# Graph attention edges on one core: the correction two steps earlier, and one wait of ScalarE in place of four

## The chip, the core and the metric

The kernel runs on one core of a Trainium2 chip. It is one program of four graph layers. The metric is the device time of one execution in microseconds; before the change it is 7833.27 us, the median of three runs (7832.72 to 7838.83).

## The reference

A graph has 6250 nodes with 256 features each and 106,250 edges, sorted by destination. Four layers follow one another, each added to its input and normalized: a mean aggregation, a gated recurrent update, a relational layer and an attention layer. The change is in the last, and there in its part over edges. After `qkv = x @ W_qkv`, with 8 heads of 32 features, it computes

```
scores = einsum("phi,phi->ph", q[src], k[dst]) / sqrt(32)
m      = segment_max(scores, src)
e      = exp(scores - m[src])
denom  = segment_sum(e, src)
w      = e / denom[src]
att    = segment_sum(w[:, :, None] * v[dst], src)
```

All data are float32. The division by `denom` comes after the sum: the kernel sums `e * v` and, in a 33rd column of each head, `e`.

## The kernel before

The edges, sorted by their node on the query side, are cut into chunks of 128, and the nodes into windows of 128. A table of 896 entries says for each entry which chunk and which window it joins; below, "chunk c" is entry c. The attention stage works through the chunks, written out without a loop (`walk(..., flat=True)`): each engine has a function `step(c, j, i)`, which is called for every c, with j = c % 32, and does its work at even c for two chunks at once. Each piece of work has a lag: it handles chunk c - lag in step c. The engines run freely and meet by semaphores, so an engine may be some steps ahead of another.

What each engine does in step c:

- ScalarE (`l3_edges_act`): copies the transposed one-hots of c - 4 out of PSUM (L1464), makes the one-hots of c - 2 out of distances (L1470); every fourth chunk copies four index columns for the gathers (L1480) and makes four key columns (L1483); makes the distances of c (L1489).
- GpSimd (`att_gather_pool`): for every chunk one indirect DMA that gathers 128 rows of keys and values, 520 numbers each (L1446). It takes the four index columns as a group. The rows have 32 slots, so chunk c takes the slot of chunk c - 32.
- TensorE (`l3_edges_pe`): transposes the one-hots of c (L1515), multiplies those of c - 2 with the query window, which gives each edge its query (L1524), and sums the weighted values of c - 26 by node with the one-hot (L1550, here called PV).
- VectorE (`l3_edges_dve`): multiplies query and key of c (L1655) and reduces by head (L1680), multiplies values with the weights for c - 22 (L1671), and adds the PV of c - 24 to the running sum of its node window (L1643), once for each of the two chunks (the row named `add`).

The maximum over the edges of a node goes across chunks, so every 16 chunks there is a batch of work on 128 x 128 scores: 16 chunks by 8 heads, transposed (L1542, L1543). VectorE scans them forward and backward (L1581, L1582) in step 0 of a batch, joins the batches by a chain of small operations on one partition in step 2 (L1596 to L1614), scans again with what was carried in and forms the difference `diff` to the maximum in step 4 (L1618 to L1621). ScalarE takes the exponential (L1496) and that of one row which corrects the sum before (L1498). TensorE transposes the exponentials into the weights (L1533) and spreads the row over the partitions by three small matmuls (L1535 to L1537). VectorE reads the weights from its step 6 on (L1671) and the row in step 8 (L1627).

The order on each engine is the order in which the steps are written. A step's waits: GpSimd's gathers of group c wait until the indices are there (`got_idx`) and until VectorE has multiplied the values of the chunks c - 32 to c - 29 (`l3["u"]`), which frees their slots. ScalarE's copy of indices waits for the gathers of the group that used the same index columns (`got3`) and for `gk`; its one-hots wait for the PV of the chunk that used the same place (`l3["pv"]`). The correction on TensorE waits for the exponentials (`p`, `cr`) and for VectorE's last reading of the previous weights (`l3["u"]`).

In the listings below the semaphores have the names under which they were first made: `n0_o` is `p`, `n0_sq` is `w`, `n0_rn` is `cr`, `n0_ss` is `arg`, `n1_aT` is `m`, `n1_hT` is `gk`, `n1_tr` is `pk`; `got_far3` is one of the `got3`.

Of the kernel before, what the change touches and what calls it, by code (L numbers as in the profile page):

```python
# [15 lines left out]
P = 128  # L16
# [3 lines left out]
NT = -(-N_NODES // P)  # L20
# [12 lines left out]
GRP = 4  # L33
# [6 lines left out]
B3 = 16  # L40
N3 = 896
R3 = 32
# [4 lines left out]
HEADS, HD = 8, 32  # L47
# [64 lines left out]
def past(c, n):  # L112

    return not isinstance(c, int) or c >= n
# [7 lines left out]
def program(nc, A, out):  # L122
    with ExitStack() as ctx:
# [1314 lines left out]
        def att_gather_pool(pool):  # L1438
            def step(c, j, i):
                g = j // GRP  # L1440
                if j % GRP == 0:
                    pool.wait_ge(got_idx, i * NG3 + g + 1)
                    if past(c, R3):
                        pool.wait_ge(l3["u"], (c + GRP - R3) // 2)
                    pool.sem_inc(s_pool, 1)
                nc.gpsimd.indirect_dma_start(  # L1446
                    out=rows3(j, 1).rearrange("p s f -> p (s f)"), out_offset=None, in_=kv_d,
                    in_offset=bass.IndirectOffsetOnAxis(ap=gidx[:, g, j % GRP:j % GRP + 1], axis=0)).then_inc(got3[g][0], 16)
            walk(pool, N3, R3, 0, step, flat=True)

        def l3_edges_act(act):
# [4 lines left out]
            def step(c, j, i):  # L1456
# [8 lines left out]
                if live(c, 2, N3):  # L1465
                    u, t, jj = i * (R3 // 2) + (j - 2) // 2, (j - 2) // 2 % 2, (j - 2) % R3
                    act.wait_ge(b3["far"], u + 1)
                    if past(c - 2, R3):
                        act.wait_ge(l3["pv"], u + 1 - R3 // 2)
                    S.activation(oh3[:, jj:jj + 2, :].rearrange("p s n -> p (s n)"), far[:, t, :], ACT.Relu,  # L1470
                                 bias=ones[:, 0:1], scale=-1.0).then_inc(b3["oh"], 1)
                if j % GRP == 0 and live(c, 0, N3):
                    g = j // GRP
                    if past(c, R3):
                        got, base = got3[g]
                        act.wait_ge(got, base + 64 * i)
                        act.wait_ge(b3["gk"], NT + (c - R3) // B3 + 1)
                    of = load_group(mybir.EngineType.Activation, chunk_i, c, GRP, NCK - 1)
                    for a in range(GRP):
                        last = S.copy(gidx[:, g, a:a + 1], idx[:, bass.ds(of[a], 1)])  # L1480
                    last.then_inc(got_idx, 1)
                    for a in range(GRP):
                        last = S.activation(pk[:, j + a:j + a + 1], keyf[:, bass.ds(of[a], 1)], ACT.Identity,  # L1483
                                            bias=nbase[:, bass.ds(c + a, 1)], scale=1.0)
                    last.then_inc(b3["pk"], 1)
                if live(c, 0, N3):
# [1 line left out]
                    for a in range(2):  # L1488
                        last = S.activation(far[:, j // 2 % 2, a * P:(a + 1) * P], iota[:, :], ACT.Abs, bias=pk[:, j + a:j + a + 1], scale=-1.0)  # L1489
                    last.then_inc(b3["far"], 1)  # L1490
                if j % B3 == 10 and batch_at(c, j, i, 10) is not None:
                    b = batch_at(c, j, i, 10)
                    act.wait_ge(b3["m"], NT + b + 1)
                    if past(b, 1):
                        act.wait_ge(b3["w"], NT + b)
                    S.activation(prob, diff, ACT.Exp, scale=SCALE).then_inc(b3["p"], 1)  # L1496
                    act.wait_ge(b3["arg"], NT + b + 1)
                    S.activation(crow, argrow, ACT.Exp, scale=SCALE).then_inc(b3["cr"], 1)  # L1498
            walk(act, N3, R3, 12, step, flat=True)

        def l3_edges_pe(pe):
            T = nc.tensor
# [3 lines left out]
            def step(c, j, i):  # L1506
# [10 lines left out]
                if live(c, 2, N3):  # L1517
# [6 lines left out]
                        last = T.matmul(ps[t][:, a * D:(a + 1) * D], ohT[:, t, a * P:(a + 1) * P],  # L1524
                                        QN[:, bass.ds(at[a], 1), :].rearrange("p a d -> p (a d)"), start=True, stop=True)
                    last.then_inc(l3["q"], 1)
                if j % B3 == 8 and batch_at(c, j, i, 8) is not None:
                    b = batch_at(c, j, i, 8)
                    hot = oh3[0:1, (j - 8 - B3) % R3, :]
                    pe.wait_ge(b3["p"], NT + b + 1)  # L1530
                    if past(b, 1):
                        pe.wait_ge(l3["u"], 8 * b)
                    T.transpose(ps[7][:, 0:P], prob, ident[:, :]).then_inc(b3["w"], 1)  # L1533
                    pe.wait_ge(b3["cr"], NT + b + 1)
                    T.matmul(ps[6][:, 0:HEADS], ones[0:1, :], ones[0:1, 0:HEADS], start=True, stop=False)  # L1535
                    T.matmul(ps[6][:, 0:HEADS], hot, minus, start=False, stop=False)
                    T.matmul(ps[6][:, 0:HEADS], hot, crow, start=False, stop=True).then_inc(b3["corr"], 1)  # L1537
                if j % B3 == 2 and batch_at(c, j, i, 2) is not None:
                    b = batch_at(c, j, i, 2)
                    pe.wait_ge(l3["s"], 8 * (b + 1))  # L1540
# [16 lines left out]
                if j % B3 == 4 and batch_at(c, j, i, 4) is not None:  # L1557
                    pe.wait_ge(b3["car"], NT + batch_at(c, j, i, 4) + 1)
                    pe.sem_inc(s_fill, 1)
                    for k in range(2):  # L1560
                        last = T.transpose(ps[6][:, k:k + 1], car[:, k, :], ident[0:1, 0:1])
                    last.then_inc(b3["col"], 1)
            walk(pe, N3, R3, LAG_PV, step, flat=True)

        def l3_edges_dve(dve, q):
# [498 lines left out]
```

## Time and profile before

| | |
|---|---|
| median of the runs | 7833.27 us |
| profiled execution | 7833.27 us, span 7831.5 us |
| TensorE, matmuls | 5394.5 us busy (69%) |
| VectorE | 5643.8 us busy (72%) |
| ScalarE | 2536.8 us busy (32%) |
| GpSimd | 3719.4 us busy (47%) |
| gathers of the attention stage | 5585.6 to 7287.6 us |
| mean granted TensorE clock | 0.834 |

The shares of the whole span are means over stages with different limits. The attention stage over edges lies between about 5580 and 7341 us. DVE is VectorE, ACT ScalarE, POOL GpSimd, PE TensorE's matmuls and PEld its weight loads; L1550 is line 1550 of the kernel before. In rows of the timeline "x4" is four instructions merged, and the bracket at the end is idle time before the row and what ended it.

### The profile page before, as it was taken

To read this page: it belongs to the slowest core of one execution; us is meant where nothing else is said; L and a number is where in the kernel's file an instruction comes from. 1 tells how busy PE (TensorE), PEld (TensorE's weight loads), DVE (VectorE), ACT (ScalarE), POOL (GpSimd) and SP (SyncE) were. 2 spreads that over 40 slices of the span, in tenths; PEclk is the share of its full clock that TensorE was granted. 3 is DMA by queue.
4 is the path that set the end of the run, shared out by engine and by line. 5 is a ranking of instruction groups with operands and counts; after the bars stand their busy time and mean duration, and the time that the engine had idled before them with its cause. 6 is when DMAs were issued, how large, how long until landed. Compare 5 with 4: busy or idle time off the path is not lost.

```text
span 7831.5 us, 119677 instructions
## 1 busy us (share of the span) xinstructions
PE 5394.5 (69%) x23535; PEld 3797.1 (48%) x23535; DVE 5643.8 (72%) x13697; ACT 2536.8 (32%) x8931; POOL 3719.4 (47%) x3949
## 2 busy tenths in 40 slices
PE   0147777773677767577747777699777777777798
PEld 0024444442344444233336666588655555555587
DVE  6857777736777777476379998711499999999666
ACT  0013323320222323011126666511355555555111
POOL 0057777711777766133347777500245544454111
PEclk9866667796666667688869999999889999999899
DMA  0023333322333333001145555555555555555211
GB/s 11 15 78 99 95 98 100 94 61 67 107 94 98 97 100 96 35 29 34 48 131 157 158 157 155 149 159 161 149 144 143 147 144 144 144 145 144 71 44 36
DMA packets 419172, 810.11 MB, mean 103 GB/s; under 512 B 74474, under 2 KB 267866, under 8 KB 418012
## 3 DMA queue, kind: packets, MB, share of 16 engines
q0 software_dynamic: 191488, 565.92, 26.3%
q1 hardware_dynamic: 224732, 230.95, 9.3%
q10 hardware_dynamic: 2304, 6.29, 0.3%
q8 instruction: 199, 3.26, 0.2%
q14 instruction: 449, 3.68, 0.2%
HBM read 680.15 MB, written 327.48 MB: 129 GB/s over the span
## 4 chain that ended last, share of the span: by engine, by line
PE 34%; DVE 32%; issue 14%; DVEq 5%; POOL 5%; DMA 4%; ACT 3%; SPq 2%; ACTq 1%; POOLq 0%
PE ps L714 7%; PE ps L1324 4%; POOL big L1210 4%; DVEq L194 4%; DVE big L1259 3%; PE ps L1550 3%; PE ps L1524 3%; DVE wreg L1643 3%; DVE ohb L661 3%; DVE big L671 2%; PE ps L1753 2%; PE ps L1770 2%; DVE big L331 2%; DVE big L332 2%; ACT big L457 2%
## 5 line engine op out<-in xcount | busy, mean ns | idle before, releaser
L714 PE MATMUL ps<-ring 128*128 x3528 | 1621.9, 595 | 872.5 <-DVE ohb L661 352.0
L714 PEld LDWEIGHTS ps<-ring 128*128 128x128 f32 x3528 | 781.5, 274 | 1374.7 <-issue 1356.1
L633 POOL DMA_INDIRECT ring<-in_x_dram,idx x832 | 834.0, 1002 | 714.9 <-DVEq L561 370.9
L695 ACT CAST ring<-ohb 128x128 f32<-128x128 bf16 x1764 | 523.4, 298 | 1864.3 <-DVE ohb L661 1830.3
L1446 POOL DMA_INDIRECT ring<-kv_d,gidx x728 | 688.5, 946 | 648.5 <-ACT gidx L1480 468.6
L633 POOL DMA_INDIRECT ring<-x_d,idx x832 | 829.0, 996 | 321.6 <-issue 229.2
L1210 POOL DMA_INDIRECT big<-x_d,idx x832 | 800.0, 962 | 349.1 <-issue 211.2
L1274 PE MATMUL ps<-big,ring 128*128 128x128 f32 x4928 | 734.9, 294 | 297.9 <-DVE big L1249 157.2
L671 DVE TENSOR_TENSOR big<-big,ps 128x257 f32 (+1 forms) x1764 | 756.7, 429 | 252.0 <-issue 87.2
L1274 PEld LDWEIGHTS ps<-big,ring 128*128 128x128 f32 x4928 | 628.7, 194 | 404.1 <-DVE big L1249 307.7
L661 DVE TENSOR_SCALAR ohb<-iotab,keyf,nbase 128x128 bf16<-128x128 bf16 x1764 | 579.8, 329 | 169.3 <-PE ps L718 80.1
L747 POOL TENSOR_TENSOR lns<-lns,neg_half 128x1 f32<-128x1 f32 x294 | 183.3, 623 | 1042.9 <-DVE lns L742 1042.9
L1550 PE MATMUL ps<-big 128*128 128x264 f32 x1792 | 559.3, 439 | 171.6 <-DVE wreg L1643 167.6
L1259 DVE SCALAR_TENSOR_TENSOR big<-big,ps 128x256 f32<-128x256 f32 x1232 | 590.1, 479 | 32.9
L1524 PE MATMUL ps<-big 128*128 x1792 | 546.8, 433 | 24.4 <-issue 8.9
L1235 ACT COPY ring<-big 128x256 f32 x1232 | 415.5, 400 | 332.7 <-POOLq L1199 191.5
L1550 PEld LDWEIGHTS ps<-big 128*128 128x128 f32 x1792 | 343.4, 209 | 346.2 <-issue 305.1
L1643 DVE SCALAR_TENSOR_TENSOR wreg<-wreg,keep,ps 128x264 f32<-128x264 f32 x840 | 402.5, 479 | 33.2 <-PE ps L1550 15.7
L1249 DVE SCALAR_TENSOR_TENSOR big<-iota,small,ring 128x128 f32<-128x128 f32 x1232 | 352.5, 347 | 76.5 <-issue 35.7
L1524 PEld LDWEIGHTS ps<-big 128*128 128x128 f32 x1792 | 348.4, 216 | 92.4 <-issue 57.3
L1324 PE MATMUL ps<-big 128*128 128x256 f32 x1568 | 358.0, 387 | 16.2 <-DMA ring<-x_d 16.2
L1464 ACT COPY big<-ps 128x256 f32<-128x256 f32 x448 | 165.1, 368 | 613.7 <-PE ps L1515 613.3
(328 smaller groups left out, 9502.1 us busy)
## 6 DMA issues: line engine op xcount, KB each, us to landing
bas_d<-big SPq DMA_DIRECT2D x1232, 128.0 KB
att_d<-wreg SPq DMA_DIRECT2D x896, 132.0 KB
big<-bas_d SPq DMA_DIRECT2D x49, 1024.0 KB, 5.6
x_d<-ring SPq DMA_DIRECT2D x147, 128.0 KB, 1.7
ring<-in_x_dram,idx POOLq DMA_INDIRECT x832
ring<-x_d,idx POOLq DMA_INDIRECT x832
big<-x_d,idx POOLq DMA_INDIRECT x832
kv_d<-ring SPq DMA_DIRECT2D x49, 260.0 KB, 2.2
```

Of the source, the lines that this page charges most:

```text
L633: nc.gpsimd.indirect_dma_start(out=rows[:, j, :], out_offset=None, in_=table, in_offset=bass.IndirectOffsetOnAxis(ap=idx_of(c), axis=0)).t ...
L661: V.tensor_scalar(ohb[:, k, :], iotab[:, :], keyf[:, bass.ds(of[k], 1)], nbase[:, q:q + 1], ALU.subtract, ALU.is_equal).then_inc(e["oh"], 1)
L671: V.tensor_tensor(here, here, ps[k][:, 0:width], ALU.add).then_inc(e["acc"], 1)
L714: T.matmul(ps[k][:, 0:D], ohf[:, k, :], rows[:, slot, :].rearrange("p a d -> p (a d)"), start=True, stop=True)
L1210: nc.gpsimd.indirect_dma_start(out=rows2[:, j, :], out_offset=None, in_=x2_d, in_offset=bass.IndirectOffsetOnAxis(ap=idx_of(c), axis=0)).t ...
L1259: V.scalar_tensor_tensor(out=cur[:, k], in0=cur[:, (k - 1) % 8], scalar=keep2[:, bass.ds(cc, 1)], in1=ps[(j - L2_LAG) % 8][:, 0:FW], op0=A ...
L1274: last = nc.tensor.matmul(ps[j % 8][:, 0:FW].rearrange("p (n h b) -> p n h b", n=NB, h=H)[:, :, h, :], xs[:, j, h * P:(h + 1) * P], wts[:, ...
L1324: last = T.matmul(ps[p][:, 0:D], basS[:, p, :, k % H, k // H], bases[:, k // H, k % H, :], start=(k == 0), stop=(k == BASES * H - 1))
L1446: nc.gpsimd.indirect_dma_start(out=rows3(j, 1).rearrange("p s f -> p (s f)"), out_offset=None, in_=kv_d, in_offset=bass.IndirectOffsetOnAx ...
L1524: last = T.matmul(ps[t][:, a * D:(a + 1) * D], ohT[:, t, a * P:(a + 1) * P], QN[:, bass.ds(at[a], 1), :].rearrange("p a d -> p (a d)"), st ...
L1550: last = T.matmul(ps[3 + a][:, 0:AV], oh3[:, jj + a, :], weighted[:, t, a * AV:(a + 1) * AV], start=True, stop=True)
L1643: V.scalar_tensor_tensor(out=acc[:, k], in0=before, scalar=keep[:, bass.ds(y, 1)], in1=ps[3 + a][:, 0:AV], op0=ALU.mult, op1=ALU.add).then ...
```

## The change

Three edits, all in the attention stage over edges.

1. GpSimd's wait for `l3["u"]` is taken out. ScalarE's waits for `got3` and `gk` at the copy of indices are taken out too, and so is the wait for `l3["pv"]` at the one-hots. In their place ScalarE waits, at the copy of indices for group c, for the PV of the chunks up to c - 29.
2. On ScalarE the exponentials are in step 8 of a batch, not in step 10.
3. On TensorE the correction (weights and row) is at the end of step 6 of a batch, not inside step 8.

```diff
--- before.py
+++ after.py
@@ -1440,8 +1440,6 @@
                 g = j // GRP
                 if j % GRP == 0:
                     pool.wait_ge(got_idx, i * NG3 + g + 1)
-                    if past(c, R3):
-                        pool.wait_ge(l3["u"], (c + GRP - R3) // 2)
                     pool.sem_inc(s_pool, 1)
                 nc.gpsimd.indirect_dma_start(
                     out=rows3(j, 1).rearrange("p s f -> p (s f)"), out_offset=None, in_=kv_d,
@@ -1465,16 +1463,12 @@
                 if live(c, 2, N3):
                     u, t, jj = i * (R3 // 2) + (j - 2) // 2, (j - 2) // 2 % 2, (j - 2) % R3
                     act.wait_ge(b3["far"], u + 1)
-                    if past(c - 2, R3):
-                        act.wait_ge(l3["pv"], u + 1 - R3 // 2)
                     S.activation(oh3[:, jj:jj + 2, :].rearrange("p s n -> p (s n)"), far[:, t, :], ACT.Relu,
                                  bias=ones[:, 0:1], scale=-1.0).then_inc(b3["oh"], 1)
                 if j % GRP == 0 and live(c, 0, N3):
                     g = j // GRP
                     if past(c, R3):
-                        got, base = got3[g]
-                        act.wait_ge(got, base + 64 * i)
-                        act.wait_ge(b3["gk"], NT + (c - R3) // B3 + 1)
+                        act.wait_ge(l3["pv"], i * (R3 // 2) + (j + GRP - R3) // 2)
                     of = load_group(mybir.EngineType.Activation, chunk_i, c, GRP, NCK - 1)
                     for a in range(GRP):
                         last = S.copy(gidx[:, g, a:a + 1], idx[:, bass.ds(of[a], 1)])
@@ -1488,15 +1482,15 @@
                     for a in range(2):
                         last = S.activation(far[:, j // 2 % 2, a * P:(a + 1) * P], iota[:, :], ACT.Abs, bias=pk[:, j + a:j + a + 1], scale=-1.0)
                     last.then_inc(b3["far"], 1)
-                if j % B3 == 10 and batch_at(c, j, i, 10) is not None:
-                    b = batch_at(c, j, i, 10)
+                if j % B3 == 8 and batch_at(c, j, i, 8) is not None:
+                    b = batch_at(c, j, i, 8)
                     act.wait_ge(b3["m"], NT + b + 1)
                     if past(b, 1):
                         act.wait_ge(b3["w"], NT + b)
                     S.activation(prob, diff, ACT.Exp, scale=SCALE).then_inc(b3["p"], 1)
                     act.wait_ge(b3["arg"], NT + b + 1)
                     S.activation(crow, argrow, ACT.Exp, scale=SCALE).then_inc(b3["cr"], 1)
-            walk(act, N3, R3, 12, step, flat=True)
+            walk(act, N3, R3, 10, step, flat=True)
 
         def l3_edges_pe(pe):
             T = nc.tensor
@@ -1524,17 +1518,6 @@
                         last = T.matmul(ps[t][:, a * D:(a + 1) * D], ohT[:, t, a * P:(a + 1) * P],
                                         QN[:, bass.ds(at[a], 1), :].rearrange("p a d -> p (a d)"), start=True, stop=True)
                     last.then_inc(l3["q"], 1)
-                if j % B3 == 8 and batch_at(c, j, i, 8) is not None:
-                    b = batch_at(c, j, i, 8)
-                    hot = oh3[0:1, (j - 8 - B3) % R3, :]
-                    pe.wait_ge(b3["p"], NT + b + 1)
-                    if past(b, 1):
-                        pe.wait_ge(l3["u"], 8 * b)
-                    T.transpose(ps[7][:, 0:P], prob, ident[:, :]).then_inc(b3["w"], 1)
-                    pe.wait_ge(b3["cr"], NT + b + 1)
-                    T.matmul(ps[6][:, 0:HEADS], ones[0:1, :], ones[0:1, 0:HEADS], start=True, stop=False)
-                    T.matmul(ps[6][:, 0:HEADS], hot, minus, start=False, stop=False)
-                    T.matmul(ps[6][:, 0:HEADS], hot, crow, start=False, stop=True).then_inc(b3["corr"], 1)
                 if j % B3 == 2 and batch_at(c, j, i, 2) is not None:
                     b = batch_at(c, j, i, 2)
                     pe.wait_ge(l3["s"], 8 * (b + 1))
@@ -1560,6 +1543,17 @@
                     for k in range(2):
                         last = T.transpose(ps[6][:, k:k + 1], car[:, k, :], ident[0:1, 0:1])
                     last.then_inc(b3["col"], 1)
+                if j % B3 == 6 and batch_at(c, j, i, 6) is not None:
+                    b = batch_at(c, j, i, 6)
+                    hot = oh3[0:1, (j - 6 - B3) % R3, :]
+                    pe.wait_ge(b3["p"], NT + b + 1)
+                    if past(b, 1):
+                        pe.wait_ge(l3["u"], 8 * b)
+                    T.transpose(ps[7][:, 0:P], prob, ident[:, :]).then_inc(b3["w"], 1)
+                    pe.wait_ge(b3["cr"], NT + b + 1)
+                    T.matmul(ps[6][:, 0:HEADS], ones[0:1, :], ones[0:1, 0:HEADS], start=True, stop=False)
+                    T.matmul(ps[6][:, 0:HEADS], hot, minus, start=False, stop=False)
+                    T.matmul(ps[6][:, 0:HEADS], hot, crow, start=False, stop=True).then_inc(b3["corr"], 1)
             walk(pe, N3, R3, LAG_PV, step, flat=True)
 
         def l3_edges_dve(dve, q):
```

TensorE, from the end of step 6 of a batch, the kernel before (L1550 is PV, L1515 the transposes of the one-hots, L1524 the query products, L1533 to L1537 the correction):

```order
L1550 MATMUL ps<-big 128x264
L1515 MATMUL ps<-ident,big 128x128 [waits l3_oht,l3_oh]
L1515 MATMUL ps<-ident,big 128x128
L194 TENSOR_LOAD chunk_tab
L1524 ISA [waits l3_prod,l3_oht]
L1524 MATMUL ps<-big 128x256
L1524 ISA
L1524 MATMUL ps<-big 128x256
L1533 MATMUL ps<-ident,wreg 128x128 [waits l3_u,n0_o]
L1535 MATMUL ps<-ones 128x8 [waits n0_rn]
L1536 MATMUL ps<-oh,big 128x8
L1537 MATMUL ps<-big 128x8
```

and the changed kernel (L1533 is now PV, L1552 to L1556 the correction, L1509 the transposes, L1518 the query products):

```order
L1533 MATMUL ps<-big 128x264
L1552 MATMUL ps<-ident,wreg 128x128 [waits l3_u,n0_o]
L1554 MATMUL ps<-ones 128x8 [waits n0_rn]
L1555 MATMUL ps<-oh,big 128x8
L1556 MATMUL ps<-big 128x8
L1509 MATMUL ps<-ident,big 128x128 [waits l3_oht,l3_oh]
L1509 MATMUL ps<-ident,big 128x128
L194 TENSOR_LOAD chunk_tab
L1518 ISA [waits l3_prod,l3_oht]
L1518 MATMUL ps<-big 128x256
L1518 ISA
L1518 MATMUL ps<-big 128x256
```

The correction stood behind the transposes and query products of step 8 and stands ahead of them now.

ScalarE, from the last distances of step 8 of a batch, the kernel before (L1464 copies the transposed one-hots, L1470 makes one-hots, L1489 distances, L1496 and L1498 are the exponentials):

```order
L1489 ACTIVATE ring<-iota,big 128x128
L1464 COPY big<-ps 128x256 [waits l3_q,l3_otr]
L1470 ACTIVATE big<-ring,ones 128x256 [waits l3_pv,l3_far]
L1489 ACTIVATE ring<-iota,big 128x128 [waits n1_tr]
L1489 ACTIVATE ring<-iota,big 128x128
L1496 ACTIVATE wreg<-wreg 128x128 [waits n0_sq,n1_aT]
L1498 ACTIVATE big<-big 1x8 [waits n0_ss]
L1464 COPY big<-ps 128x256 [waits l3_q,l3_otr]
```

and the changed kernel (L1462 copies, L1466 one-hots, L1483 distances, L1490 and L1492 exponentials):

```order
L1483 ACTIVATE ring<-iota,big 128x128
L1490 ACTIVATE wreg<-wreg 128x128 [waits n0_sq,n1_aT]
L1492 ACTIVATE big<-big 1x8 [waits n0_ss]
L1462 COPY big<-ps 128x256 [waits l3_q,l3_otr]
L1466 ACTIVATE big<-ring,ones 128x256 [waits l3_far]
L1483 ACTIVATE ring<-iota,big 128x128 [waits n1_tr]
L1483 ACTIVATE ring<-iota,big 128x128
L1462 COPY big<-ps 128x256 [waits l3_q,l3_otr]
```

The exponentials have moved ahead of the copy, the one-hots and the distances of step 10.

ScalarE, the next copy of indices in a batch (step 12), the kernel before (L194 loads four table values into registers, L1480 copies the index columns):

```order
L1470 ACTIVATE big<-ring,ones 128x256 [waits l3_pv,l3_far]
L194 TENSOR_LOAD chunk_tab [waits n1_hT,got_far3]
L1480 ISA
L1480 COPY gidx<-idx 128x1
L1480 ISA
```

and the changed kernel (L1474 copies the index columns):

```order
L1466 ACTIVATE big<-ring,ones 128x256 [waits l3_far]
L194 TENSOR_LOAD chunk_tab [waits l3_pv]
L1474 ISA
L1474 COPY gidx<-idx 128x1
L1474 ISA
```

The wait for PV has moved from the one-hots to the register load, and the waits for `gk` and the old gathers are gone.

## Rows read from the trace of the kernel before

**Rows 1.** Windows: stretch, length, busy us (instructions) by engine, granted clock, DMA share, GB/s.

```profile
5700.00:7300.00 1600.00, 1187.58 (x4960) 833.36 (x4958) 1481.51 (x3503) 835.38 (x3422) 785.62 (x831) 0.91 0.53 144
6540.00:6545.00 5.00, 4.08 (x11) 3.05 (x12) 3.98 (x13) 1.36 (x4) 1.75 (x2) 0.57 0.60 163
6551.00:6563.00 12.00, 9.32 (x42) 6.68 (x43) 11.73 (x25) 8.24 (x34) 7.56 (x8) 1.00 0.69 196
```

**Rows 2.** Waits of VectorE, 5700 to 7300 us: us in total, times, longest.

```profile
DVE big L1655 <- PE ps L1524: 48.3, 104, 1.3
DVE big L1655 <- DMA ring<-kv_d,gidx: 5.9, 9, 1.2
```

**Rows 3.** Source line of the exponentials: duration min/median/max, first and last start.

```profile
L1496 ACT ACTIVATE wreg<-wreg x56: 309/309/310, 5628.4 to 7309.0; 128x128 f32<-128x128 f32 x56
```

**Rows 4.** Timeline of VectorE in one batch: start, us, engine, line, operation.

```profile
6532.40 0.68 DVE L1655 TENSOR_TENSOR big<-ps,ring 128x512 f32<-128x512 f32 x1
...
6546.38 0.69 DVE L1671 TENSOR_TENSOR big<-big,ps 128x528 f32<-128x528 f32 x1
...
6548.38 0.68 DVE L1655 TENSOR_TENSOR big<-ps,ring 128x512 f32<-128x512 f32 x1
...
6549.78 0.49 DVE L1643 SCALAR_TENSOR_TENSOR wreg<-wreg,keep,ps 128x264 f32<-128x264 f32 x1
...
6551.18 0.68 DVE L1655 TENSOR_TENSOR big<-ps,ring 128x512 f32<-128x512 f32 x1
...
6554.24 0.68 DVE L1655 TENSOR_TENSOR big<-ps,big 128x512 f32<-128x512 f32 x1
...
6557.04 0.68 DVE L1655 TENSOR_TENSOR big<-ps,big 128x512 f32<-128x512 f32 x1
...
6562.80 0.68 DVE L1655 TENSOR_TENSOR big<-ps,ring 128x512 f32<-128x512 f32 x1
```

**Rows 5.** Timeline of TensorE: the same batch.

```profile
6540.90 0.34 PE L1561 MATMUL ps<-ident,iota_q 1*128 1x1 f32 x2 [3.16 <-DVE iota_q L1610]
...
6543.74 1.97 PE L1550 MATMUL ps<-big 128*128 128x264 f32 x4
6545.50 0.64 PE L1515 MATMUL ps<-ident,big 128*128 128x128 f32 x2
6545.93 1.84 PE L1524 MATMUL ps<-big 128*128 x4
6547.61 0.27 PE L1533 MATMUL ps<-ident,wreg 128*128 128x128 f32 x1
...
6548.61 1.13 PE L1550 MATMUL ps<-big 128*128 128x264 f32 x4
6549.57 0.38 PE L1515 MATMUL ps<-ident,big 128*128 128x128 f32 x2
6549.79 1.03 PE L1524 MATMUL ps<-big 128*128 x4
...
6554.47 1.13 PE L1550 MATMUL ps<-big 128*128 128x264 f32 x4 [0.82 <-DVE wreg L1643]
```

**Rows 6.** Timeline of ScalarE in the same batch.

```profile
6546.50 0.31 ACT L1496 ACTIVATE wreg<-wreg 128x128 f32<-128x128 f32 x1 [3.24 <-DVE wreg L1621]
...
6547.48 0.45 ACT L1480 COPY gidx<-idx 128x1 int32 x4
```

**Rows 7.** Chain that ended last, around one late group of gathers: start, us, what.

```profile
6644.24 0.31 ACTq L194
...
6644.80 0.09 ACT gidx L1480
...
6649.81 4.58 DMA ring<-kv_d,gidx
```

**Rows 8.** Timeline at the start of the stage: a last gather, VectorE's next product.

```profile
5599.40 0.94 POOL L1446 DMA_INDIRECT ring<-kv_d,gidx  x1 [0.30 <-issue]
...
5603.22 0.69 DVE L1655 TENSOR_TENSOR big<-ps,ring 128x512 f32<-128x512 f32 x1 [1.59 <-DMA ring<-kv_d,gidx]
```

## Prediction

> **What bounds the kernel now.** Read the windows of the attention stage first. Between 5700 and 7300 us VectorE is busy for 1481.5 of 1600 us, TensorE for 1187.6, ScalarE for 835.4, GpSimd for 785.6, and the DMA engines for about half of the time [rows 1]. VectorE bounds the stage, by some 93%. The waits say how much a better order could give: in these 1600 us VectorE waited 48.3 us for the query products (L1524) and 5.9 us for gathered rows [rows 2]. Only the stage is touched: its 56 batches start 1680.6 us apart from first to last, 30.6 us each [rows 3]. I work on one batch, from VectorE's product at 6532.40 us to the one at 6562.80 us, 30.40 us, close to that mean [rows 4].
>
> A word on names. "Step c" is what an engine does for loop index c, two chunks at a time, and c is counted from the batch's start (0, 2, ... 14, then 16 = the next 0). VectorE's product of step c needs the query product of c, which TensorE makes in its step c+2. VectorE's first accumulate of step c needs the value product ("PV") of TensorE's step c+2. The "correction" is the transpose of the probabilities and the three small matmuls (L1533 to L1537 of before).
>
> In the batch, step 6 of VectorE starts at 6548.38, its first accumulate at 6549.78, and steps 8, 10, 12 and 16 start at 6551.18, 6554.24, 6557.04 and 6562.80 [rows 4].
>
> **The correction, two steps earlier on TensorE and ScalarE.** First what releases it. ScalarE's exponential starts at 6546.50, after a wait for VectorE's difference, not for its own queue [rows 6]. All 56 of them have to wait for that, and moving the exponential ahead in ScalarE's queue can't start it earlier. The transpose also waits for VectorE to have read the previous batch's weights, the multiply of step 4, which runs from 6546.38 to 6547.07 [rows 4]. So in the new order too the correction can't start before 6547.07.
>
> Today TensorE uses that waiting time: in step 8 it does the one-hot transposes (6545.50) and the query products (6545.93, 1.84 us), then the correction at 6547.61, then PV at 6548.61 [rows 5]. In the new order the correction stands ahead of those two. TensorE ends the PV of step 6 at 6545.71 [rows 5], stands still until 6547.07, and does the correction in 1.0 us (6547.61 to 6548.61 today) until 6548.1. Only then come transposes and query products. They take 1.25 us at the full clock (6549.57 to 6550.82) or 2.27 us at the half clock (6545.50 to 6547.77) [rows 5]. ScalarE's new order doesn't hold them up further: today too the exponentials are followed by a copy and a one-hot, and it is through with those at 6547.48, when the copy of indices starts [rows 6].
>
> So VectorE's product of step 6 starts at 6549.35 or 6550.4 instead of 6548.38. What counts is the first accumulate. At the full clock PV runs from about 6549.2 for 1.13 us, VectorE needs 1.2 us for product and multiply, and the accumulate is at 6550.6, against 6549.78: 0.8 us later. At the half clock the PV takes 2.0 us [rows 5] and ends at 6552.2: 2.4 us later. Which clock? TensorE had stood still for 3.16 us until 6540.90 [rows 5], and the granted clock from 6540 to 6545 was 0.57 of full, that is mostly the 1.2 GHz level; from 6551 to 6563 it was 1.00, that is 2.4 GHz [rows 1]. The new order adds an idle stretch of 1.4 us where the clock is just coming back, so both will be seen. I take the middle, 1.6 us a batch, and keep 0.8 and 2.4 as ends. In 56 batches: 90 us (45 to 134). Nothing behind it absorbs it: the correction feeds the accumulate of step 8, which VectorE reaches later anyway.
>
> **The gather's gate.** GpSimd no longer waits for the multiply that frees a row slot, and ScalarE's index copy for group c (chunks c to c+3) now waits for a PV. Both guard the same chunks, c-32 to c-29. But the multiply of c-30 is VectorE's step c-8, while its PV is TensorE's step c-4. The gate opens some four to six chunks later. Behind the waiting instruction in ScalarE's queue are the keys, the distance and one-hot of the next chunks, behind them in GpSimd's the four gathers.
>
> How long from gate to data? The chain of one group where the data came late: register load at 6644.24, index copy at 6644.80, the last of the four gathers issued at 6649.81, landed 4.58 us later: 10.15 us from load to landing [rows 7]. At the start of the stage a last gather, issued at 5599.40, let VectorE go on at 5603.22, after 3.82 us [rows 8]. With 3.82 it is 9.4 us, with 0.1 us to pass the semaphore 9.5. I take 9.5, and keep 9.1 (a landing 0.4 us quicker than that row) and 10.25 (the slow group).
>
> The Trainium skill, page "DMA: Bandwidth & Descriptors", section "Anatomy of one DMA — SWDGE (gpsimd) path", fits 2.0 us plus the bytes at 436 GB/s for a GpSimd DMA; for the 260 KB of one gather that is an estimate of 2.6 us. The trace disagrees (3.82 and 4.58); by the page each group would be there 1.2 us sooner and the term below would fall to some 60 us. The skill's page "Runtime: NRT & Kernel Launch", section "Instruction fetch mechanics", gives about 200 ns for each register loaded; by it the four registers of a group cost 0.8 us, an estimate, where the trace shows 0.56 us from the load to the copy [rows 7], and the term would grow by some 13 us.
>
> Now against the need, group by group. Group 16: its gate is the PV of step 12, which starts 0.23 us after VectorE's product of step 10 (6554.24 and 6554.47) and takes 1.13 us [rows 4, 5]. Its data are there 1.36 + 9.5 = 10.86 us after that product. VectorE wants them at 6562.80, 8.56 us after it. Missing: 2.3 us. Group 12: its gate is the PV of step 8, whose end is at the first accumulate of step 6 or up to 0.2 us ahead; from there to the product of step 12 are 7.26 us (6549.78 to 6557.04) [rows 4], up to 7.5, against 9.5. Missing: 2.1 us. The two are not added: a stall before step 12 also gives group 16 its time, so both together cost 2.3 us. Groups 4 and 8 have the long chain steps 0 to 6 of VectorE ahead (6532.40 to 6551.18 is 18.8 us for eight chunks) and are in time. With 9.1 us it is 1.9, with 10.25 it is 3.05. The first 32 chunks have no gate, so 54 batches: 124 us (103 to 165). This hides what VectorE waits for gathers today, 5.9 us in the window [rows 2], about 7 in the stage.
>
> **Sum.** 90 + 124 - 7 = 207 us on a span of 7831.5 gives 8038.5. The median of the runs is 7833.27, 1.8 us above the profiled span, so the forecast is 8040 us. The terms do add: the correction delays the PV that opens gate 12, it doesn't overlap with the time behind it. By the ends of both terms: 45 + 103 - 7 = 141 and 134 + 165 - 7 = 292, so 7974 to 8125; a half-speed PV at the gates would add up to 0.9 us in a batch, hence 8150 as the upper end.
>
> **Rivals.**
> 1. Only the correction costs; the gathers are in time after all, because their landing is nearer 2 us where the queue is not full, or because VectorE's own delay gives them room. For it: VectorE waited for gathers only 9 times on ring slots in 1600 us [rows 2]. Against: these waits come with a gate that opens four chunks sooner. 7833 + 90 = 7923 us.
> 2. Only the gate costs; the correction finds idle time, TensorE runs fast, and VectorE's first accumulate, which waits for PV anyway, moves by nothing. For it: it holds if the query product of step 6 were ready before the correction's releaser; against: it stands behind it in the queue. 7833 + 117 = 7950 us.
> 3. No change: both waits were implied by others. For it: PV of the same chunks was already waited for by ScalarE in its next step but one or so (L1470). Against: that wait asks for two chunks fewer and two steps earlier work. 7833 us.
> 4. Faster. The mechanism is in steps 6 to 8: with the correction out of TensorE's step 8 its PV follows the query products at once, and VectorE's waits for L1524 shrink. It decides if the correction's operands are ready before TensorE has ended step 6. The price is bounded by the waits, 48.3 us [rows 2]; if half of them went, and all of the 7 us for gathers with GpSimd's freed wait, that is 31 us: 7802 us. Against it is the difference that releases the exponential, later than the end of step 6 in the row.
>
> **How the numbers follow.** Both costs 0.68; rival 1 0.09; rival 2 0.08; rival 3 0.07; rival 4 0.08. What this kernel's measurement can tell from no change is about 0.2%, 16 us. Slower by over 0.2%: 0.68 + 0.09 + 0.08 = 0.85; within: 0.07; faster: 0.08. The likeliest case's own range is 7970 to 8150. To hold the time 8 times in 10 I extend it down to 7915, which takes in rivals 1 and 2.
>
> **What the changed profile would show.** Right: on TensorE the correction's transpose waits over 1 us for ScalarE or VectorE in most batches, with the one-hot transposes and query products right behind it; VectorE waits for L1518 at step 6; new VectorE waits for gathered rows of about 2 us once in a batch, at chunk 12 (and little at 16); GpSimd waits for the index copy, ScalarE's register load for PV; a batch of 34.3 us. Its busy times stay. Wrong: if VectorE's waits for gathers stay at a few us, the gate's term is gone; if the product of step 6 follows its predecessor without a wait, the correction's term is gone. Wrong in size: a landing time near 2 us, or a TensorE clock that stays at one level in steps 6 to 8.

## The result and the profile after

The changed kernel takes 8121.76 us (8115.53 to 8129.23, 4 runs) against 7836.05 us for the kernel before, measured with it: ratio 1.0361, 95% interval 1.0342 to 1.0379. By the medians that is 286 us slower; 207 us were forecast, and the forecast of 8040 us is 82 us short. The span of the profiled execution is 8115.3 us.

The busy times of the stage have not changed, only its length. Windows of the changed kernel, from 5700 us until nearly all chunks are through (answers to rows 1; columns as there):

```profile
5700.00:7560.00 1860.00, 1331.84 (x4930) 904.48 (x4928) 1482.62 (x3483) 836.87 (x3430) 792.41 (x832) 0.85 0.45 123
```

VectorE's 1482.62 us are the 1481.51 of rows 1, but in 1860 us and not 1600. The exponentials' source line (answers to rows 3):

```profile
L1490 ACT ACTIVATE wreg<-wreg x56: 309/309/310, 5623.6 to 7592.0; 128x128 f32<-128x128 f32 x56
```

(7592.0 - 5623.6) / 55 is 35.8 us a batch, against 30.6: 5.2 us more. The waits of the changed kernel, 5700 to 7570 us (answers to rows 2; total us, times, longest; L1518 makes the query products, L1533 is PV, L1552 the correction's transpose):

```profile
ACT gidx L1474 <- PE ps L1533: 553.2, 209, 4.3
...
DVE big L1649 <- PE ps L1518: 206.7, 217, 2.9
...
PE ps L1552 <- DVE big L1665: 85.9, 52, 2.1
...
DVE big L1649 <- DMA ring<-kv_d,gidx: 65.7, 69, 2.1
...
DVE big L1649 <- DMA big<-kv_d,gidx: 39.3, 26, 2.3
...
PE ps L1509 <- ACT big L1466: 24.7, 73, 0.6
```

VectorE waits 206.7 us for query products (48.3 before) and 105.0 us for gathered rows (6.6 before, both kinds of slots). The correction waits for VectorE, as forecast, and ScalarE waits 553.2 us at its new gate. The last row is new too: TensorE waits for one-hots (L1466) behind that gate, 24.7 us in 73 times, a wait that the kernel before does not have between 5700 and 7300 us. One batch on VectorE, in the timeline of the changed kernel (answers to rows 4; steps 2, 4, 6, the first accumulate of step 6, steps 8, 10, 12, 14 and 16):

```profile
6512.21 0.69 DVE L1649 TENSOR_TENSOR big<-ps,ring 128x512 f32<-128x512 f32 x1 [0.18 <-PE ps L1518]
...
6519.62 0.69 DVE L1649 TENSOR_TENSOR big<-ps,ring 128x512 f32<-128x512 f32 x1 [0.68 <-PE ps L1518]
...
6526.08 0.69 DVE L1649 TENSOR_TENSOR big<-ps,ring 128x512 f32<-128x512 f32 x1 [2.05 <-PE ps L1518]
...
6527.82 0.49 DVE L1637 SCALAR_TENSOR_TENSOR wreg<-wreg,keep,ps 128x264 f32<-128x264 f32 x1 [0.44 <-PE ps L1533]
...
6529.22 0.68 DVE L1649 TENSOR_TENSOR big<-ps,ring 128x512 f32<-128x512 f32 x1
...
6532.85 0.69 DVE L1649 TENSOR_TENSOR big<-ps,ring 128x512 f32<-128x512 f32 x1 [0.49 <-PE ps L1518]
...
6537.02 0.69 DVE L1649 TENSOR_TENSOR big<-ps,ring 128x512 f32<-128x512 f32 x1 [1.48 <-DMA ring<-kv_d,gidx]
...
6539.64 0.68 DVE L1649 TENSOR_TENSOR big<-ps,ring 128x512 f32<-128x512 f32 x1
...
6542.85 0.69 DVE L1649 TENSOR_TENSOR big<-ps,ring 128x512 f32<-128x512 f32 x1 [0.18 <-DMA ring<-kv_d,gidx]
```

Read the brackets: 2.05 us for the product of step 6 and 0.44 us for the PV behind it, then 0.49 us for the product of step 10, and 1.48 and 0.18 us for gathered rows at steps 12 and 16. TensorE in the same batch (answers to rows 5):

```profile
6522.79 0.30 PE L1552 MATMUL ps<-ident,wreg 128*128 128x128 f32 x1 [1.68 <-DVE big L1665]
...
6523.48 0.36 PE L1556 MATMUL ps<-big 1*128 1x8 f32 x2
6523.78 0.44 PE L1509 MATMUL ps<-ident,big 128*128 128x128 f32 x2
6524.07 1.97 PE L1518 MATMUL ps<-big 128*128 x4
6525.83 1.95 PE L1533 MATMUL ps<-big 128*128 128x264 f32 x4
```

The correction starts at 6522.79 and takes 1.0 us, as at the full clock in rows 5. The query product follows it, at 6524.07, in 1.97 us: the half clock. And the gate: ScalarE's copy of indices and GpSimd's first and fourth gather of group 12.

```profile
6528.23 0.47 ACT L1474 COPY gidx<-idx 128x1 int32 x4 [3.20 <-PE ps L1533]
...
6529.51 0.94 POOL L1444 DMA_INDIRECT ring<-kv_d,gidx  x1 [9.50 <-ACT gidx L1474]
...
6533.25 0.95 POOL L1444 DMA_INDIRECT ring<-kv_d,gidx  x1 [0.30 <-issue]
```

PV ended at 6527.78 (6525.83 + 1.95), the rows were there at 6537.02: 9.24 us, where I took 9.5.

### The profile page after: what moved, and what is told of

It reads as the page before. It is cut to its first block, busy times and chain, and to the rows that moved or that the text cites. A ratio compares the mean times of both kernels' runs of the same rounds, so it can differ in the third digit from the quotient of the medians.

```text
span 8115.3 us, 119026 instructions
## 1 busy us (share of the span) xinstructions
PE 5523.2 (68%) x23532; PEld 3865.2 (48%) x23535; DVE 5655.8 (70%) x13697; ACT 2539.4 (31%) x8931; POOL 3722.7 (46%) x3949
## 3 DMA queue, kind: packets, MB, share of 16 engines
q0 software_dynamic: 191488, 565.92, 25.2%
## 4 chain that ended last, share of the span: by engine, by line
PE 33%; DVE 30%; issue 13%; DMA 6%; POOL 5%; DVEq 5%; ACT 4%; SPq 2%; ACTq 1%; POOLq 0%
PE ps L714 6%; PE ps L1324 4%; PE ps L1518 4%; DVE big L1259 4%; DVEq L194 4%; POOL big L1210 3%; DVE ohb L661 3%; DMA ring<-kv_d,gidx 2%; DVE big L671 2%; PE ps L1747 2%; PE ps L1764 2%; PE ps L1533 2%; DVE big L331 2%; POOL ring L1444 2%; DVE big L332 2%
## 5 line engine op out<-in xcount | busy, mean ns | idle before, releaser
L1533 PE MATMUL ps<-big 128*128 128x264 f32 x1792 | 597.9, 465 | 135.3 <-DVE wreg L1637 131.2
L1518 PE MATMUL ps<-big 128*128 x1792 | 605.8, 471 | 61.5 <-issue 37.8
L1533 PEld LDWEIGHTS ps<-big 128*128 128x128 f32 x1792 | 384.8, 229 | 309.4 <-issue 247.3
L1649 DVE TENSOR_TENSOR big<-ps,ring 128x512 f32<-128x512 f32 x364 | 251.2, 690 | 308.1 <-PE ps L1518 213.2
L1518 PEld LDWEIGHTS ps<-big 128*128 128x128 f32 x1792 | 376.3, 233 | 159.7 <-issue 118.0
L1637 DVE SCALAR_TENSOR_TENSOR wreg<-wreg,keep,ps 128x264 f32<-128x264 f32 x840 | 402.7, 479 | 37.4 <-PE ps L1533 35.3
```

Source lines behind the costliest of these rows:

```text
L1533: last = T.matmul(ps[3 + a][:, 0:AV], oh3[:, jj + a, :], weighted[:, t, a * AV:(a + 1) * AV], start=True, stop=True)
```

## The experiments

Theory A is the prediction's: two costs, the order of the correction on TensorE and the late gate, here with the sizes read from the trace after. Differences in us are the change of the ratio times 7834 us, with the 95% interval of the ratio; differences of the medians lie up to 7 us from them (e1 +190, e2 +138). "Us a batch" is read from the first and last start of the exponentials, as in rows 3; it was 30.6 before.

| kernel | against before | ratio | us a batch |
|---|---|---|---|
| changed kernel | +283 | 1.0342 to 1.0379 | 35.8 |
| correction alone (e1) | +197 | 1.0234 to 1.0268 | 33.9 |
| gate alone (e2) | +143 | 1.0166 to 1.0200 | 33.0 |
| gate opened by the multiply (e3) | 0 | 0.9991 to 1.0010 | 30.5 |
| correction on TensorE alone (e4) | +187 | 1.0222 to 1.0257 | 34.0 |
| exponentials on ScalarE alone (e5) | +256 | 1.0309 to 1.0344 | 35.3 |
| GpSimd waits for PV (e6) | +76 | 1.0080 to 1.0113 | 31.9 |
| changed kernel, gaps filled (e7) | +178 | 1.0210 to 1.0244 | 33.7 |
| before, gap filled (e8) | -11 | 0.9976 to 0.9996 | 30.3 |
| e1, gaps filled (e9) | +31 | 1.0025 to 1.0052 | 31.2 |
| carries later (e10) | +5 | 0.9999 to 1.0016 | 30.6 |
| carries and rows later (e11) | +1 | 0.9992 to 1.0009 | 30.7 |
| e10, gaps filled (e12) | -20 | 0.9960 to 0.9987 | (other chip) |

**The correction alone (e1).** Edits 2 and 3 of the change without edit 1.

> The kernel before with the correction moved on TensorE and ScalarE alone; all waits of the gathers as before. Theory A (two costs that add; in the trace of the changed kernel VectorE waits about 2.05 us for the query product of step 6 and 0.44 us for the PV behind it, at the half clock, in every batch): +2.5 us in each of 56 batches, about +140 us, and hardly any wait of VectorE for gathers. Theory B (the gate is the main cost, the correction is slow only because ScalarE and TensorE are already late from the gate): under +60 us.

Measured +197 us: neither theory's number, though the place is A's. VectorE waits 215.0 us for query products over the whole stage (57.7 before) and 31.5 us for gathers (31.1 before). VectorE in one batch of e1 (the multiply of step 4, the product of step 6, its first accumulate, the product of step 8):

```profile
6539.97 0.69 DVE L1671 TENSOR_TENSOR big<-ring,ps 128x528 f32<-128x528 f32 x1
...
6544.99 0.69 DVE L1655 TENSOR_TENSOR big<-ps,ring 128x512 f32<-128x512 f32 x1 [2.94 <-PE ps L1524]
...
6546.75 0.49 DVE L1643 SCALAR_TENSOR_TENSOR wreg<-wreg,keep,ps 128x264 f32<-128x264 f32 x1 [0.46 <-PE ps L1539]
...
6548.47 0.69 DVE L1655 TENSOR_TENSOR big<-ps,ring 128x512 f32<-128x512 f32 x1 [0.23 <-PE ps L1524]
```

and TensorE (L1558 to L1562 are the correction, L1539 PV), with the windows of the stretch from the carries' transposes to the half-speed products (the granted clock is the third number from the end):

```profile
6540.81 0.45 PE L1558 MATMUL ps<-ident,wreg 128*128 128x128 f32 x1 [1.51 <-DVE big L1671]
...
6542.06 0.57 PE L1562 MATMUL ps<-big 1*128 1x8 f32 x2
6542.56 0.69 PE L1515 MATMUL ps<-ident,big 128*128 128x128 f32 x2
6543.04 1.91 PE L1524 MATMUL ps<-big 128*128 x4
6544.75 1.97 PE L1539 MATMUL ps<-big 128*128 128x264 f32 x4
```

```profile
6534.50:6546.90 12.40, 10.88 (x31) 7.99 (x32) 7.99 (x20) 4.24 (x18) 2.29 (x3) 0.50 0.24 71
```

The clock is 0.50 for the whole of it. From the multiply (6539.97) the product of step 6 is 5.02 us away; in rows 4 it is 2.00 (6546.38 to 6548.38). The correction itself takes 1.75 us here (6540.81 to 6542.56), not 1.0.

**The gate alone (e2).** Edit 1 of the change without the others.

> The kernel before with the waits of the gathers changed alone; the correction where it was. Theory A: what is left of the 285 us, about +140 us (2.6 us in 54 batches): waits of VectorE for gathered rows of some 100 us in all and some 0.5 us a batch for the query product of step 10, whose one-hots ScalarE makes late. Theory B: over +220 us. The two kernels' gains should sum to about the 285 us if the costs are independent; if the sum is well under, they share a cause.

Measured +143 us, as A. VectorE's idle time before its product, over the whole stage of e2, by what ended it:

```profile
  DMA ring<-kv_d,gidx: 91.8, 69
  PE ps L1518: 89.0, 169
  DMA big<-kv_d,gidx: 43.3, 27
```

Before it was 31.1 us for gathers and 57.7 us for query products over the whole stage: 104 us of the cost are gathers, 31 us query products. The two kernels' costs sum to 340 us, 57 more than the change (42 more by the medians, 27 more by the spans of the profiled executions): some of the two is shared. The gathers' part is not: VectorE waits 135.5 us for gathered rows over the changed kernel's stage and 135.1 us in e2. What is shared lies in the waits for TensorE. Those for query products grow by 157 us in e1 and by 31 us in e2, but by 168 us in the changed kernel (225.3 for 57.7), and those for PV by 22, 5 and 20 us. In e1 the wait for the product of step 6 is 2.94 us, in the changed kernel 2.05 in the batch shown, where the correction took 1.0 us (6522.79 to 6523.78) and only the work behind it went at the half clock. Over all 56 batches the correction's transpose takes 305 ns in the changed kernel and 448 ns in e1 (medians). Why the clock differs there was not settled.

**What opens the gate (e3).** In e3 GpSimd's wait is gone, and

```diff
-                        got, base = got3[g]
-                        act.wait_ge(got, base + 64 * i)
-                        act.wait_ge(b3["gk"], NT + (c - R3) // B3 + 1)
+                        act.wait_ge(l3["u"], i * (R3 // 2) + (j + GRP - R3) // 2)
```

> The kernel before, in which GpSimd's wait is taken out and ScalarE waits at the copy of indices for the multiply (which frees the row slots) instead of the old gathers and the keys; the one-hots' wait for PV stays. One wait in ScalarE's queue, but it opens at VectorE's step c-8, not with PV. Theory A (it is when the gate opens that costs): within 20 us of before, 0 to +20. Rival (it is that ScalarE, not GpSimd, waits, with the one-hots queued behind it): +60 us or more.

Measured no difference. One wait on ScalarE in place of GpSimd's, `got3` and `gk` costs nothing if it opens with the multiply.

**GpSimd waits for PV (e6).** In `att_gather_pool`:

```diff
-                        pool.wait_ge(l3["u"], (c + GRP - R3) // 2)
+                        pool.wait_ge(l3["pv"], (c + GRP - R3) // 2)
```

> The kernel before with one word changed: GpSimd waits for PV instead of the multiply of the same chunks. ScalarE's waits stay. Theory A: the gate opens as late as in the changed kernel, but register load and copy of indices are done before it, so a group is 1.8 us sooner than there: about 8.2 us from the end of PV to the data against 9.5 before, VectorE short of some 1.0 us a batch, +55 us, and no wait for one-hots. Rival (what matters is the gate's time alone): as the gate on ScalarE.

Measured +76 us, half of e2: nearer A's 55 than the rival's number. All of it is gathers: VectorE waits 105.7 us for them over the stage, 74.6 more than before, and the waits for query products don't grow (54.8 for 57.7). The expectation's step was off (1.8 us sooner than 9.5 is 7.7, not 8.2), and in one batch the data of group 12 were there 8.69 us after PV's end (6559.18 to 6567.87), later than both. With e3 this settles the gate's term: it is when the gate opens, and what of the 9.5 us lies behind it.

**Which engine's order (e4, e5).** e4 has the diff of `l3_edges_pe` alone, e5 that of the exponentials alone.

> The kernel before with the correction moved on TensorE alone; the exponentials stay in ScalarE's step 10. Theory A (TensorE's order is the cost, since the transposes and query products of step 8 stand behind a wait that ends at the same time): as with both moved, about +140 us. Rival (the cost is ScalarE's: the exponentials ahead of the copy and one-hots that the query product needs): near 0.

Measured +187 us, the same as e1 within the intervals: TensorE's order alone is the whole of e1.

> The kernel before with the exponentials in ScalarE's step 8 alone; the correction stays in TensorE's step 8, behind the query product of step 6, which now needs a copy that stands behind the exponentials. Theory A: the query product can't start before the exponentials' end, so product of step 6 comes late as well: +60 to +140 us. Rival (only TensorE's order counts): within 20 us of before.

Measured +256 us, more than either theory gave. TensorE in one batch of e5 (transposes, query product, correction, PV):

```profile
6518.53 0.44 PE L1515 MATMUL ps<-ident,big 128*128 128x128 f32 x2 [1.55 <-ACT big L1470]
6519.33 1.13 PE L1524 MATMUL ps<-big 128*128 x4 [0.36 <-issue]
6520.29 0.27 PE L1533 MATMUL ps<-ident,wreg 128*128 128x128 f32 x1
...
6521.76 2.13 PE L1550 MATMUL ps<-big 128*128 128x264 f32 x4
```

and VectorE (the product of step 6 and its first accumulate):

```profile
6520.49 0.69 DVE L1655 TENSOR_TENSOR big<-ps,ring 128x512 f32<-128x512 f32 x1 [1.12 <-PE ps L1524]
...
6523.93 0.49 DVE L1643 SCALAR_TENSOR_TENSOR wreg<-wreg,keep,ps 128x264 f32<-128x264 f32 x1 [2.14 <-PE ps L1550]
```

The transposes wait 1.55 us for one-hots that stand behind the exponentials, and then transposes, query product, correction and PV stand in a row. The first two run near the full clock (0.44 and 1.13 us), the correction takes 1.5 us (6520.29 to 6521.76) and PV runs at the half clock; it ends at 6523.89. My price left out the PV behind them: over the stage VectorE's waits for query products grow by 132 us (190.1 for 57.7) and those for PV by 125 us (141.2 for 16.7), together the measured cost. In the change the correction stands ahead of the transposes and waits for the exponentials itself, and e1, which has both moves, costs no more than e4: this cost doesn't come on top.

**The clock (e7, e8, e9).** Matmuls whose results are not used keep TensorE busy ahead of two waits; in e8 only the first kind:

```diff
+                    for _ in range(10):
+                        T.matmul(ps[5][:, 2 * P:3 * P], ident[:, :], ones[:, :], start=True, stop=True)
                     pe.wait_ge(b3["car"], NT + batch_at(c, j, i, 4) + 1)
...
+                    pe.wait_ge(l3["prod"], min(i * (R3 // 2) + j // 2 - 1, N3 // 2))
+                    for _ in range(6):
+                        T.matmul(ps[j // 2 % 2][:, 0:P], ident[:, :], ones[:, :], start=True, stop=True)
                     pe.wait_ge(b3["p"], NT + b + 1)
```

> The changed kernel with 10 more matmuls of 128x128 ahead of TensorE's wait for the carries and 6 ahead of the correction, whose results are not used. They only keep TensorE busy where it would stand still. Theory A (half of the correction's 2.5 us is the half clock after these idle stretches): the waits for the query products of steps 4 and 6 shrink by some 1.5 to 2 us a batch, 80 to 110 us faster than the changed kernel, about 8020 us. Rival (the clock is not set by these gaps, or the fill is itself in the way): no change or slower.

Measured 105 us faster than the changed kernel (+178 against +283), as A. The waits for query products fell from 225.3 to 123.2 us over the stage, 1.8 us a batch.

> The kernel before with 10 more matmuls of 128x128, results not used, ahead of TensorE's wait for the carries in step 4 of a batch. Theory A: the transposes and query product behind that wait run at the full clock, VectorE's wait of 0.7 us for the product of step 4 goes: 30 to 50 us faster than before, about 7795 us. Rival (VectorE is the bound and other waits take its place): within 15 us of before.

Measured -11 us: a small gain, in the rival's range and at most a third of what A gave. The waits for query products fell from 57.7 to 35.9 us over the stage, and those for PV rose from 16.7 to 25.2: part of the wait moved, as the rival says.

> The kernel of the first run (correction moved on TensorE and ScalarE alone, +190 us) with 10 more matmuls of 128x128 ahead of the wait for the carries and 6 ahead of the correction, results not used. In that run's trace the correction, transposes and query product after it take 4.2 us at the half clock, where rows at the full clock give 2.25. Theory A (the order costs about 1.0 to 1.2 us a batch and the half clock the rest): +55 to +80 us over before. Rival (the order alone costs the 3.4 us, TensorE is slow for another reason): +170 us or more.

Measured +31 us, below A's range and far from the rival's. The order that costs 197 us costs 31 with TensorE kept busy. Windows of e9, and its timeline around the correction (fill, correction, transposes, query product, PV):

```profile
5700.00:7300.00 1600.00, 1260.49 (x6515) 951.33 (x6515) 1453.23 (x3439) 823.69 (x3398) 779.56 (x826) 0.99 0.52 142
```

```profile
6533.26 2.20 PE L1559 MATMUL ps<-ones,ident 128*128 128x128 f32 x12
6535.30 0.27 PE L1563 MATMUL ps<-ident,wreg 128*128 128x128 f32 x1
...
6536.26 0.44 PE L1515 MATMUL ps<-ident,big 128*128 128x128 f32 x2
6536.53 1.03 PE L1524 MATMUL ps<-big 128*128 x4
6537.40 1.05 PE L1539 MATMUL ps<-big 128*128 128x264 f32 x4
```

The granted clock is 0.99 over the stage, and from the correction to the end of the query product it is 2.26 us (6535.30 to 6537.56), where e1 has 4.14. Against e8, which has the first fill too, the order costs 42 us (29 to 55, by the two intervals), 0.75 us a batch; that is near the 0.8 us that the prediction worked out for the full clock. It can hold some cost of the second fill: in the batch shown VectorE's multiply ended at 6534.37 and the correction started only behind the fill, at 6535.30, though in most batches (45 of 56) it still waited for VectorE. Both kernels fill the old gap ahead of the carries as well as the new one, and e1 with only one of them filled was not run. So it is shown that the order costs little when the clock is up, and not which of the two gaps keeps it down.

**The other direction (e10, e11, e12).** In e10 the block of the carries' transposes stands, with 6 for 4 in its conditions, behind the query product:

```diff
+                if j % B3 == 6 and batch_at(c, j, i, 6) is not None:
+                    pe.wait_ge(b3["car"], NT + batch_at(c, j, i, 6) + 1)
```

> The kernel before with another move: TensorE's two small transposes of the carries (L1561), which wait for VectorE's chain, go from the end of step 4 into step 6, behind the transposes of one-hots and the query product of step 4, which need nothing of the chain. The opposite of the change's order: work that is ready goes ahead of the wait. Theory A: TensorE does that work in the 3.2 us in which it stands still, VectorE's wait of 0.73 us for the product of step 4 goes, 56 x 0.7 = 40 us faster than before: about 7795 us. Rival (the small transposes come later and the chain grows by as much): no change.

Measured no difference (+5), the rival's number. VectorE's waits in e10 (5700 to 7300 us), and TensorE (L1531 are the carries' transposes, L1556 is PV, L1539 the correction's transpose):

```profile
DVE wreg L1643 <- PE ps L1556: 45.6, 52, 1.0
DVE big L1655 <- PE ps L1524: 9.7, 52, 0.3
```

```profile
6525.24 0.25 PE L1531 MATMUL ps<-ident,iota_q 1*128 1x1 f32 x2 [2.08 <-DVE iota_q L1610]
6527.81 1.57 PE L1556 MATMUL ps<-big 128*128 128x264 f32 x4 [2.31 <-DVE wreg L1643]
...
6531.31 0.42 PE L1539 MATMUL ps<-ident,wreg 128*128 128x128 f32 x1
```

The wait for query products is gone (9.7 us for 48.3), and a wait of 45.6 us for PV is there, which was 1.0 before in the same window. How much of the missing gain is the rival's longer chain was not measured. The rows show that the gap moved: TensorE stands still 2.31 us ahead of PV, and PV takes 1.57 us, the product behind it 1.92.

e11 moves the rows' transposes in the same way.

> As the run before it, and the four transposes of the chain's rows (L1555) too go behind the transposes and the query product of the next step. Theory A: VectorE's wait of 0.17 us for the product of step 2 goes too: some 10 us faster than the run before it, about 7785 us. Rival: the query product, 1.0 us, now stands ahead of the four transposes that VectorE's chain waits for, and the chain starts later: slower than the run before it.

Measured +1: no difference either, neither A's gain nor the rival's loss. Again the wait moved: over the stage VectorE waits 3.1 us for query products (15.0 in e10) and 77.6 us for PV (62.3 in e10).

e12 is e10 with 8 such matmuls ahead of and 8 behind the carries' transposes.

> The kernel with the carries' transposes later (no change in time: VectorE's wait for the query product went, but TensorE stood still for 2.1 us ahead of the transposes and 2.3 us behind them, and its PV and the correction at the half clock made VectorE wait anew), with 8 matmuls of 128x128, results not used, in each of these two gaps. Theory A (the half clock behind the gaps made the new wait): the correction's steps run at the full clock, VectorE's waits for TensorE fall under 20 us in the stage, 30 to 60 us faster than before, about 7790 us. Rival (VectorE's own work is the bound and the waits come back elsewhere, for gathered rows above all): within 15 us of before.

Measured ratio 0.9974 (0.9960 to 0.9987): some 20 us faster, between the two theories. This run was on a chip where it takes 8727 us and the kernel before 8753, so only the ratio is used; there is no trace of the kernel before on that chip to compare its waits with, so A's "under 20 us" of waits stays open. It has the lowest ratio of all versions, but its interval overlaps with that of e8 (0.9976 to 0.9996).

## Why the prediction came out as it did

**What bounds the kernel, and the sign**: right. VectorE's busy time stayed, and the stage grew by VectorE's waits.

**The gate's term, 124 us less 7**: right in mechanism and nearly in size (e2: +143; 9.24 us from gate to data against 9.5). The step that fell short is "ScalarE's queue behind the wait": I named keys, distances and one-hots there and priced none. They cost the 0.49 us at step 10 and 31 us of waits for query products in e2; TensorE's waits for one-hots (L1466) point at them, but no run took them apart from the gathers except e6, where ScalarE has no late gate and these waits don't grow. The gathers themselves cost 104 us, less than the 117. The last gather of group 12 took 3.77 us (6533.25 to 6537.02), as in rows 8. The estimate of 2.6 us by the Trainium skill, page "DMA: Bandwidth & Descriptors", section "Anatomy of one DMA — SWDGE (gpsimd) path", doesn't hold for it; the trace decides.

**The correction's term, 90 us**: right in mechanism, wrong in size; of the steps this is the one that failed. "Does the correction in 1.0 us" took the full clock, and "I take the middle" of 0.8 and 2.4 us took the two clock levels as equally likely. Alone the edit costs 3.5 us a batch (e1, 197 us in 56 batches; 3.3 by the starts of the batches), beyond my upper end of 2.4, since correction, transposes, query product and PV all run at the half clock, and the correction itself takes 1.75 us. With the clock kept up (e9 against e8) it costs 0.75. So three quarters or more of it are the half clock. I had that as a choice between two rows, for the work behind the correction alone, and not as the likely state of the whole stretch from the correction to PV: the idle 1.4 us come right after a stretch at 0.57. That the new gap itself keeps the clock down is not shown.

**The sum**: "the terms do add" was not quite so. Alone they sum to 340 us, together they are 283. My two mis-sizings, too small on the correction and a little on the gate, were partly made good by that. The measured time is in the likeliest case's range (7970 to 8150) and in the stated one, but by luck in part: with the correction sized as in e1 and terms that add, the prediction's own way gives 7833 + 340 = 8173 us, above that range.

**The rivals**: 1 and 2 (one cost alone) fall, since e1 and e2 each cost over 140 us. 3 and 4 fall with the sign.

## What to carry to other kernels

On an engine that works in order, put what is ready ahead of what must wait; moving a step forward whose releaser doesn't move gains nothing and holds up all behind it. Before one wait replaces several, write down the step at which each opens and what of a transfer's chain lies behind it: the same chunks guarded by a later consumer cost 143 us here, by the earlier one nothing. For the upper end of a range, price a new idle gap on TensorE with all that follows it at the half clock, up to the row where the clock is back, and not only with the wait.

## What the runs showed of the hardware that was not expected

- In this stage TensorE's granted clock was 0.91 before, 0.85 in the changed kernel and 0.99 in e9, where it is kept busy with unused work. That work made the changed kernel 105 us and e1 some 166 us faster, but the kernel before, with the first of the two fills, only 11 us, though its granted clock rose from 0.91 to 0.96: where VectorE was the bound, a faster TensorE mostly moved the wait.
- In e1 the clock stayed at its lower level (0.50) for 12.4 us in which TensorE was busy for 10.88, with one gap of 1.5 us inside. In the changed kernel's batch, with a gap of 1.68 us at the same place, the correction behind it ran at the full clock and the query products behind that at the half. The length of a gap alone did not tell which it would be.
